# A two-layer AdaLN network on one core: half-chunks at the start of a block, paired products in a correction

## The reference, cut to what matters

```
q = x@Wq + bq;  k = x@Wk + bk;  v = x@Wv + bv
Q = elu(q) + 1; K = elu(k) + 1
KV = sum over tokens of K*v;  Ksum = sum over tokens of K
V = Q * KV / (Q*Ksum + 1e-6)
attn = gelu(V@Wo + bo)
x = layernorm(attn + x) * ln1_s + ln1_b
h = gelu(x@Wf1 + bf1);  ff = gelu(h@Wf2 + bf2)
x = layernorm(ff + x) * ln2_s + ln2_b
```

## Time and profile before

| | us |
|---|---|
| runs | 1975.67, 1970.92, 1968.33 |
| median | 1970.92 |
| profiled execution | 1969.74 |
| its span | 1968.0 |
| TensorE busy | 1720.7 (87%) |
| VectorE busy | 1353.3 (69%) |
| ScalarE busy | 1137.2 (58%) |
| GpSimd busy | 285.7 (15%) |

### The profile page before, as it was taken

How to read it: one execution, slowest core, us unless ns; L and a number is a source line. 1 busy time by engine, 2 the same in 40 slices (tenths; PEclk the granted TensorE clock), 3 DMA queues, 4 the chain that set the end, 5 groups by cost and what they waited for, 6 DMA issues and landing times.

```text
span 1968.0 us, 28168 instructions
## 1 busy us (share of the span) xinstructions
PE 1720.7 (87%) x10420; PEld 770.0 (39%) x10420; DVE 1353.3 (69%) x2656; ACT 1137.2 (58%) x2091; POOL 285.7 (15%) x364
## 2 busy tenths in 40 slices
PE   5898139699999999999979988999989998799999
PEld 4788137122222222222234434444444444444443
DVE  6998876899999999999724356565665656522222
ACT  5465003279989999998863345665566655222222
POOL 4456001400000000000000011111111111111111
PEclk8999658589999999999989989999999999799999
DMA  1000000122100000000012320000000000312441
GB/s 51 1 1 1 0 0 2 39 38 35 17 2 2 2 2 2 2 2 2 18 28 52 91 41 1 17 17 2 15 17 17 17 0 1 43 34 49 48 56 31
DMA packets 72528, 39.12 MB, mean 20 GB/s; under 512 B 22113, under 2 KB 68705, under 8 KB 72401
## 3 DMA queue, kind: packets, MB, share of 16 engines
q1 hardware_dynamic: 71824, 36.65, 10.4%
q10 hardware_dynamic: 576, 0.79, 0.1%
HBM read 34.08 MB, written 3.15 MB: 19 GB/s over the span
## 4 chain that ended last, share of the span: by engine, by line
PE 60%; DVE 28%; ACT 4%; issue 3%; DMA 2%; POOL 1%; SPq 1%; DVEq 0%; ACTq 0%; POOLq 0%
DVE MX L1144 17%; PE PS L1711 6%; PE PS L1226 6%; PE PS L1717 6%; PE PS L2226 4%; PE PS L2227 4%; PE PS L2236 4%; PE PS L1662 4%; PE PS L1252 4%; PE PS L539 3%; PE PS L1681 2%; PE PS L1103 2%; PE PS L1819 2%; DMA SB<-scr_w 2%; DVE MS L643 2%
## 5 line engine op out<-in xcount | busy, mean ns | idle before, releaser
L1285 ACT ACTIVATE tmpb<-PS 128x512 f32<-128x512 f32 x1024 | 554.1, 595 | 76.1 <-PE PS L1252 56.9
L1144 DVE TENSOR_REDUCE MX<-PS 128x2 f32<-128x1024 f32 x512 | 584.5, 1216 | 17.8 <-PE PS L1103 15.9
L1226 PE MATMUL PS<-tmpb,VS 128*32 128x256 f32 x4096 | 327.8, 392 | 1.5 <-ACT tmpb L1285 0.6
L1103 PE MATMUL PS<-KST,QST 56*128 56x512 bf16 x1024 | 205.4, 399 | 18.5 <-DVE MX L1144 16.7
L1252 PE MATMUL PS<-QST,KST 59*128 59x512 bf16 x1024 | 200.6, 388 | 3.8 <-ACT tmpb L1285 1.0
L2261 DVE TENSOR_TENSOR HG<-HG,PS 128x512 f32<-128x512 f32 (+1 forms) x96 | 65.9, 686 | 183.1 <-PE PS L2227 183.1
L2251 ACT ACTIVATE HG<-PS 128x512 f32<-128x512 f32 (+1 forms) x96 | 57.2, 595 | 186.6 <-PE PS L2226 186.6
L1226 PEld LDWEIGHTS PS<-tmpb,VS 128*32 128x32 f32 x4096 | 80.8, 108 | 195.9 <-issue 108.4
L1252 PEld LDWEIGHTS PS<-QST,KST 59*128 59x128 bf16 x1024 | 49.5, 93 | 222.5 <-ACT tmpb L1285 209.0
L1711 PE MATMUL PS<-X,WF 128*128 128x512 f32 x256 | 124.3, 620 | 3.8 <-ACT X L1907 3.7
L1923 ACT ACTIVATE HF<-PS,CL 128x512 f32<-128x512 f32 x128 | 87.9, 687 | 64.6 <-PE PS L1711 64.6
(11 more groups left out here) (335 smaller groups left out, 2528.6 us busy)
## 6 DMA issues: line engine op xcount, KB each, us to landing
SB<-scr_w SPq DMA_DIRECT2D x14, 1024.0 KB, 14.6
WF<-in_L_attn_Wf SPq DMA_DIRECT2D x16, 256.0 KB, 3.1
QST<-NMP SPq DMA_DIRECT2D x192, 1.0 KB
G<-in_L_ffn_w SPq DMA_DIRECT2D x16, 176.0 KB, 2.4
W<-in_L_ffn_w SPq DMA_DIRECT2D x16, 128.0 KB, 2.2
QST<-scr_q SPq DMA_DIRECT2D x14, 128.0 KB
scr_q<-tmpb SPq DMA_DIRECT2D x3, 512.0 KB, 3.6
KST<-scr_k SPq DMA_DIRECT2D x14, 96.0 KB
```

Source lines behind the costliest of these rows:

```text
L1103: pe.matmul(PS[:, b + x, :], QST[r, 2 * g + jj, CH * qc + P * t:CH * qc + P * t + P], KST[r, g, cs(kc)], start=True, stop=True).then_inc(s ...
L1144: r = v.tensor_reduce(MX[:, :, m // (TPC * NC), m // NC % TPC, m % NC], PS[:, b:b + 2, :], AX.X, ALU.max)
L1226: last = pe.matmul(PS[32 * j:32 * j + 32, 3, h], VS[:, kt, u // NC, :], PB[:, kt % 2, j, h], start=(kt == 0 and half == 0), stop=(kt == NT ...
L1285: a.activation(PB[:, kt % 2, j, :], PS[:, at % 3, :], ACT.Exp, scale=HD ** -0.5).then_inc(s_exp, 1)
```

## The change

Two edits in two places.

**Correction.** For every second tile (`paired`) VectorE adds the upper four slices onto the lower four, a sum of 512 elements per row in the same buffer, and TensorE adds up four slices instead of eight.

**Blocks.** Chunk 0 goes from the tanh to the scale and bias in two halves of 256 columns, each with a semaphore step of its own: tanh, projection, gelu, sum, turn (two transposes each), statistics (two of the four), apply and turn back (two each), scale and bias. The halves use two banks: the second half of the projection goes to bank 6, of the turn to bank 0, of the turn back to bank 6. On TensorE the turn of chunk 0 now stands before the projection of chunk 1. The aggregates, the epsilon and the power stay whole. `WARM` is 5. The counts of the semaphores follow: a side-1 counter (`upto1`) has five steps a block instead of four. The second norm is unchanged.

```diff
+        def paired(s):
+            return s % 2 == 1
         def pe_corr(pe, s):
+            n = HD // 2 if paired(s) else HD
...
-            for j in range(HD):
+            for j in range(n):
...
+                m = v.tensor_tensor(CP[s % 3], O[:, s, :, HD:SCOL]...to_broadcast([P, HD, H0, HD]), S0t[:, :, :, :], ALU.mult)
+                if paired(s):
+                    chain.link(m)
+                    h = HD // 2
+                    m = v.tensor_tensor(CP[s % 3][:, 0:h, :, :], CP[s % 3][:, 0:h, :, :], CP[s % 3][:, h:HD, :, :], ALU.add)
+                m.then_inc(s_cp, 1)
...
-        WARM = 6
+        WARM = 5
+        HC, OBANK0B = CH // 2, 6
...
+        def upto1(n):
+            return n + n // NC + 2
...
         def pe_wo(pe, b, c):
+            if c == 0:
+                pe.wait_ge(s_vv, upto1(NC * b) - 1)
+                pe.matmul(PS[:, OBANK[0], 0:HC], WO2[:, :], Q1[:, 0:HC], start=True, stop=True).then_inc(s_wo, 1)
+                pe.wait_ge(s_vv, upto1(NC * b))
+                pe.matmul(PS[:, OBANK0B, 0:HC], WO2[:, :], Q1[:, HC:CH], start=True, stop=True).then_inc(s_wo, 1)
+                return
...
+        def pe_turn_halves(pe, banks, src, ready, count, done):
+            pe.wait_ge(ready, count - 1)
+            for j in range(TPC):
+                if j == TPC // 2:
+                    x.then_inc(done, 1)
+                    pe.wait_ge(ready, count)
+                x = pe.transpose(PS[:, banks[2 * j // TPC], P * j:P * j + P], src[:, P * j:P * j + P], ident[:, :])
+            x.then_inc(done, 1)
...
         def pe_t1(pe, n):
+            if n % NC == 0:
+                pe_turn_halves(pe, (1, 0), Y1, s_y1, upto1(n), s_t1)
+                return
...
         def pe_u1(pe, n):
+            if n % NC == 0:
+                pe_turn_halves(pe, (2, 6), flat(N1), s_n1, upto1(n), s_u1)
+                return
...
             pe_wo(pe, b, 0)
+            pe_t1(pe, n)
             pe_wo(pe, b, 1)
-            pe_t1(pe, n)
...
         def act_v(a, b, c):
+            if c == 0:
+                a.activation(Q1[:, 0:HC], Q1[:, 0:HC], ACT.Tanh, scale=0.5, bias=lnz1[:, 0:1]).then_inc(s_vv, 1)
+                a.activation(Q1[:, HC:CH], Q1[:, HC:CH], ACT.Tanh, scale=0.5, bias=lnz1[:, 0:1]).then_inc(s_vv, 1)
+                return
...
         def act_g1(a, b, c):
+            if c == 0:
+                a.wait_ge(s_wo, upto1(NC * b) - 1)
+                a.wait_ge(s_bo, b + 1)
+                a.activation(ZR[:, 0, 0:HC], PS[:, OBANK[0], 0:HC], ACT.Gelu_apprx_tanh, bias=GB[:, 0:1]).then_inc(s_g1, 1)
+                a.wait_ge(s_wo, upto1(NC * b))
+                a.activation(ZR[:, 0, HC:CH], PS[:, OBANK0B, 0:HC], ACT.Gelu_apprx_tanh, bias=GB[:, 0:1]).then_inc(s_g1, 1)
+                return
...
         def act_x1(a, b, c):
+            if c == 0:
+                if n >= 2:
+                    a.wait_ge(s_y2, upto2(n - 1 - 1))
+                a.wait_ge(s_u1, upto1(NC * b) - 1)
+                a.activation(X1[:, n % 2, 0:HC], PS[:, 2, 0:HC], ACT.Identity, scale=col(b, C1), bias=col(b, B1))
+                a.wait_ge(s_u1, upto1(n))
+                a.activation(X1[:, n % 2, HC:CH], PS[:, 6, HC:CH], ACT.Identity, scale=col(b, C1), bias=col(b, B1)).then_inc(s_bx1, 1)
+                return
...
         def v_y1(v, b, c):
+            if c == 0:
+                v.wait_ge(s_g1, upto1(NC * b) - 1)
+                v.tensor_tensor(Y1[:, 0:HC], ZR[:, 0, 0:HC], HT[:, 0:HC], ALU.add).then_inc(s_y1, 1)
+                v.wait_ge(s_g1, upto1(n))
+                v.tensor_tensor(Y1[:, HC:CH], ZR[:, 0, HC:CH], HT[:, HC:CH], ALU.add).then_inc(s_y1, 1)
+                return
...
+                if halves and j == TPC // 2:
+                    v.wait_ge(turned, counts(side)(n))
+                x = v.bn_stats(BS[:, side, j, :], PS[:, banks[2 * j // TPC], P * j:P * j + P])
...
+                if halves and j == TPC // 2 - 1:
+                    x.then_inc(done, 1)
             x.then_inc(done, 1)
```

More of the change, by code:

```diff
@@ L656, in pe_corr @@
             pe.wait_ge(s_cp, s + 1)
-            for j in range(HD):
-                last = pe.matmul(o, ident[:, :], CP[s % 3][:, j, :, :].rearrange("p h c -> p (h c)"), start=False, stop=j == HD - 1,
+            for j in range(n):
+                last = pe.matmul(o, ident[:, :], CP[s % 3][:, j, :, :].rearrange("p h c -> p (h c)"), start=False, stop=j == n - 1,
                                  skip_group_check=True)
@@ L715, in act_out, with v_corr @@
             act_ht(a, 3)
-        def v_corr(v, c):
+        def v_corr(v, chain, c):
             for s in tiles(c):
@@ L746, in v_out @@
             v.wait_ge(s_ov, NT)
-            v_corr(v, 0)
-            v_corr(v, 1)
+            v_corr(v, chain, 0)
+            v_corr(v, chain, 1)
             v_sums(v, chain, 0)
-            v_corr(v, 2)
+            v_corr(v, chain, 2)
             v_scale(v, chain, 0)
             v_sums(v, chain, 1)
-            v_corr(v, 3)
+            v_corr(v, chain, 3)
             v_scale(v, chain, 1)
@@ L1979, in v_inputs @@
             if b:
-                v_stats(v, chain, 1, 6, s_t2, s_ep2, n - 1)
+                v_stats(v, chain, 1, (6, 6), s_t2, s_ep2, n - 1)
             v_p(v, chain, b, 0)
             if b:
-                v_apply(v, 1, 6, N2, s_r2, s_u2, s_n2, n - 1)
+                v_apply(v, 1, (6, 6), N2, s_r2, s_u2, s_n2, n - 1)
             v_k(v, chain, b, 0)
@@ L2005, in v_y1, with v_stats @@
             n = NC * b + c
-            v.wait_ge(s_g1, n + 1)
+            if c == 0:
+                if n:
+                    v.wait_ge(s_t1, upto1(n - 1))
+                v.wait_ge(s_g1, upto1(NC * b) - 1)
[3 more added lines that the diff above has]
+                return
+            v.wait_ge(s_g1, upto1(n))
             if n:
-                v.wait_ge(s_t1, n)
+                v.wait_ge(s_t1, upto1(n - 1))
             v.tensor_tensor(Y1[:, :], ZR[:, c, :], HT[:, cs(c)], ALU.add).then_inc(s_y1, 1)
-        def v_stats(v, chain, side, bank, turned, done, n):
-            v.wait_ge(turned, n + 1)
+        def v_stats(v, chain, side, banks, turned, done, n, halves=False):
+            v.wait_ge(turned, counts(side)(n) - (1 if halves else 0))
             for j in range(TPC):
-                x = v.bn_stats(BS[:, side, j, :], PS[:, bank, P * j:P * j + P])
+                if halves and j == TPC // 2:
+                    v.wait_ge(turned, counts(side)(n))
+                x = v.bn_stats(BS[:, side, j, :], PS[:, banks[2 * j // TPC], P * j:P * j + P])
             chain.link(x)
@@ L2019, in v_stats, with v_apply @@
             v.tensor_scalar(VE[:, side, :], BA[:, side, :, 1], 1e-6, None, ALU.add).then_inc(done, 1)
-        def v_apply(v, side, bank, N, rstd, used, done, n):
+        def v_apply(v, side, banks, N, rstd, used, done, n, halves=False):
             v.wait_ge(rstd, n + 1)
             if n:
-                v.wait_ge(used, n)
+                v.wait_ge(used, n if side else upto1(n - 1))
             for j in range(TPC):
-                x = v.tensor_scalar(N[:, j, :], PS[:, bank, P * j:P * j + P], BA[:, side, j, 0:1], RR[:, side, j:j + 1],
+                x = v.tensor_scalar(N[:, j, :], PS[:, banks[2 * j // TPC], P * j:P * j + P], BA[:, side, j, 0:1], RR[:, side, j:j + 1],
                                     ALU.subtract, ALU.mult)
+                if halves and j == TPC // 2 - 1:
+                    x.then_inc(done, 1)
             x.then_inc(done, 1)
         def v_first(v, chain, n):
-            v_stats(v, chain, 0, 1, s_t1, s_ep1, n)
+            v_stats(v, chain, 0, (1, 0) if n % NC == 0 else (1, 1), s_t1, s_ep1, n, n % NC == 0)
         def v_body(v, chain, b):
@@ L2042, in v_body @@
                 if m:
-                    v_stats(v, chain, 1, 6, s_t2, s_ep2, n + m - 1)
+                    v_stats(v, chain, 1, (6, 6), s_t2, s_ep2, n + m - 1)
                 if m + 2 < NC:
```

42 lines of the change are left out of this document (23 added, 19 removed).

## The result

| | before | after |
|---|---|---|
| median of the runs, us | 1973.3 (4 runs, 1968.3 to 1976.2) | 1944.62 (4 runs, 1943.6 to 1946.2) |
| ratio, 95% interval | | 0.9861 (0.984 to 0.9881) |
| profiled execution, us | 1969.74 | 1943.64 |
| its span, us | 1968.0 | 1941.8 |

The change is 28.7 us faster by the medians and 26.2 by the two spans. The prediction was 1950, range 1943 to 1960. It was added up from the profiled 1969.74; the median of before had been 1970.92 then and is 1973.3 with a fourth run.

A forecast was written before the change was run, and what follows sets the result against it. TensorE carries 60% of the chain and VectorE 28%; VectorE bounds the softmax stage, TensorE the layer-1 blocks, whose starts are serial. 5.2 + 12.8 + 2.6 = 20.6 us off 1969.74 gives 1949.1, predicted as 1950, range 1943 to 1960.

The forecast's parts named there:

- Correction, 5.2: Layer 0's correction: odd tiles get 5 TensorE products instead of 9, VectorE pays eight sums; 5.2 us less.
- the walk: Step-by-step timing of the correction stage with VectorE as bound, ending at 310.0 instead of 315.17.
- Halves, 12.8: Start of the eight layer-1 bodies: chunk 0 by halves brings the feed-forward 1.6 us earlier each, 12.8 us.
- A cost per instruction speaks against halves: Block start: the skill's objection that small tiles expose a fixed cost; the measured slope's 0.23 us was already counted.
- Warm products, 0: Ahead of each body: five unread products instead of six gain 0, hidden behind VectorE's chain to the weight.
- Clock, 2.6: First feed-forwards of two blocks ran slow at 1.2 GHz; shorter TensorE idle stretches would end this, 2.6 us.
- rival 2: Block starts: the clock's fall moves instead of going; hitting all eight blocks gives 1960 us; chance 0.08.
- Rival 1: Block starts: VectorE and ScalarE queues each 0.4 later, 1956 us; halves as dear as wholes, 1962; chance 0.17 together.
- Rival 3: Block starts: clock falls at the body's start and stays low until the feed-forward's end; 1976 us, chance 0.05.
- Rival 4: Correction gives nothing because VectorE's sum costs as much as it frees; 1954 us, chance 0.06.

The follow-up runs named there:

- filled: Kernel before plus three unread 512-column products on TensorE between projection 3 and the turn back of chunk 0; 1965.94 us, ratio 0.9957.
- blocks_only: Changed kernel with no correction tile paired, so only the blocks changed; 1951.19 us, ratio 0.989 to the kernel before.
- again: The changed kernel itself run once more, in a second set of five runs; 1946.55 us, ratio 0.9878 to the kernel before.
- tanh3_early: Changed kernel with tanh 3 ahead of gelu 1 on ScalarE; 1944.73 us, ratio 0.9863 to the kernel before.
- warm6: Changed kernel with six unread products before the body instead of five; 1948.70 us, ratio 0.9872 to the kernel before.
- corr_only: Kernel before with only the correction paired for odd tiles, blocks as before; 1966.01 us, ratio 0.9967.
- order_only: Kernel before with only chunk 0's turn put ahead of projection 1 on TensorE, no halves; 1971.06 us, ratio 0.9998.
- wo1_first: Changed kernel with TensorE's old order, projection 1 ahead of chunk 0's turn; 1959.76 us, ratio 0.9931 to the kernel before.
- warm0: Changed kernel with no unread products before the body instead of five; 1964.71 us, ratio 0.9948 to the kernel before.
- wo1_filled: Changed kernel with projection 1 ahead of chunk 0's turn and two unread products between projection 3 and the turn back; 1947.88 us, ratio 0.9879.

## Why the prediction was right, step by step

The sign, the places and the range were right. The size was 20.6 us against 28.7 by the medians. The medians can be taken apart in steps: from before to `filled`, which removes the falls only, 7.4 us (8.5 by its own ratio); from `filled` to `blocks_only`, which has the halves, the new order, five unread products ahead instead of six and no fillers, 14.8; from there to the changed kernel, which differs in the pairing alone, 6.6, or 4.6 to `again`. Together 28.7. Since these medians come from different chips, the profiles price the halves and the correction better.

- **Correction, 5.2.** Measured 6.1 on the mean of the stages, 6.7 in the two profiles. The mechanism was right in that fewer products on TensorE are paid for by VectorE until VectorE is the limit. With every tile paired it is (`all_paired`); with every second one the two engines are level, so the walk, which had VectorE as the bound alone, went a little too far. Its prices were a little high. I took 0.74 for a sum and 1.23 for a product; in the row at 302.37 the next product begins 0.60 behind the sum's start, before the sum has ended; the sum itself, which is linked to the product ahead of it, begins only after that product's end (302.33). The walk ended at 31.5 us and the stage at 30.3.
- **Halves, 12.8.** Measured 14.1 (8 × 1.76). The walked lead was 1.6 a block. Half prices were near: gelu 0.45 (0.455), sum 0.42 (0.43), the two scalings together 1.01 (0.92). The error of 0.2 sits in the two queues that the apply waits for. I let the power collide with sum 1 and take 1.25 to 1.4; it took 1.01. And sum 1 ended 5.54 us behind the first tanh instead of the walked 5.73, since its gelu ran 0.2 earlier. In the earlier trace rows sum 1 already runs when the power begins (1389.65 and 1389.82), which I called lying inside it; in the changed kernel it begins 0.33 us after the power has, overlaps it for 0.68 us and lengthens it by nothing. The level queues are there as walked: power and sum 1 end 0.01 us apart. On ScalarE gelu 3 holds the scaling up by 0.2, which `tanh3_early` gives back.
- **A cost per instruction speaks against halves.** The measured halves agree with the slope of the earlier trace rows, 0.455 against 0.45, and not with the lower 0.36, an estimate by the table of the Trainium skill ("VectorE: DVE Perf Modes", the TRN2 errata section). Its advice against small tiles did not decide here: two half gelus took 0.82 us from the start of the first to the end of the second against 0.69 for a whole one, but the first half, for which the sum waits, was done 0.24 earlier than a whole one.
- **Warm products, 0.** `warm6`: 0.09 a block, 0.7 in all.
- **Clock, 2.6.** This is the term that was mis-sized. 2.6 is what the profiled execution of before had lost, and the profiles agree on it (14.9 − 7 × 1.76 = 2.6). The runs lose more, 7 to 9 us by `filled`: about 5 to 6 of the 8.1 us by which the sum fell short. It was read from one execution, and the loss differs between executions: `corr_only` lost 4.8 with the same blocks. The prediction said that the moment decides, in rival 2, and did not conclude that the profile's 2.6 was itself one case of many. It also argued from the length of TensorE's idle stretches, which did shrink to 0.76 us; `order_only` and `wo1_first` show that idle length is not what decides.
- **Rival 1** (level queues, 0.4 each later): did not happen; the queue on VectorE cost nothing and the one on ScalarE 0.2. **Rival 2** (the fall moves): did not happen to this kernel, 0 falls in all 40 bodies of `after`, `again`, `blocks_only`, `all_paired` and `warm6`. It happened to its neighbour `wo1_first`, at 9.7 us, near the 10.4 that rival 2 priced for all eight blocks. **Rival 3** (clock down from the body's start): not with five products; with none, 2.3 a block. **Rival 4**: no.
- **The rest.** 3.2 us of the two profiles' difference lie where nothing was changed (first and third rows of the table of stretches). They are inside the spread of 4.6 us that equal instructions showed, so I take them as luck of this pair of profiles and not as a gain of the change. With `again`, whose profile begins the blocks 1.6 us later, they are 1.7.

One thing stays open: the exact condition under which the clock falls. The column "transposes only" separates the kernels (`warm0`, whose clock fell elsewhere, apart): none of the 72 bodies with 1.6 to 2.4 us fell, and in the four kernels with 2.9 to 4.4 us 17 of 32 did. Within the four it gives no order: 4.4 us went with two and three falls, 3.4 with seven, and these are counts of one profile each. Idle time does not separate them: `order_only` and `wo1_first` idle for 1.5 us at most and fall more often than the kernel before with its 2.75. That fits the Trainium skill ("TensorE: Matmul & The Clock Gate", Part 4: transposes do not count as activity like other products) and its Part 1 (the monitor's window does not start with the kernel), by which equal bodies can differ, as two of eight did in the kernel before. No run here replaced the transposes themselves, so it was not shown that they are the cause; that products in the stretch end the falls was shown, by `filled` and `wo1_filled`.

## What to carry to other kernels

Where one chain crosses several engines and all of them idle, price the halves by the slope between two sizes of the same operation in the trace, and then walk each engine's queue: the lead is what the later of two queues leaves. When TensorE has idle stretches, read what it does in them and where its real products stand, not only how long it idles; an order that looks 0.2 us worse or better can cost or save 10 us by the clock. A loss by the clock read in one profile is one case of many, so count it as a range, and look at the spread of the runs of before.

## What the runs showed of the hardware that I had not expected

- Whether projection 3 ends 4.9 us behind the bias product (`wo1_first`) or 6.3 (the changed kernel) went with seven falls or none: 9.7 us. In `tanh3_early` it ends at 5.5, and none fell.
- In `wo1_first` the falls followed one another: the first feed-forwards went from 4.79 to 5.38 us, the spacing settled at 61.4, and every body behind the first one that fell did too. That a fall brings on the next was not tested.
- Kernels with equal instructions ahead of the blocks reach them at 1187.75 to 1192.3 us. In the two profiles at the ends, the changed kernel and `wo1_first`, the correction's first product was already 1.5 us apart (277.4 and 278.9); from 190.8 to 194.2 the granted clock was 1.00 in the first and 0.50 in the second.
- GpSimd's power of four columns takes 1.01 us where VectorE is at rest when it begins (176 of 176 such powers in the fourteen profiles). Where VectorE's sum of two SBUF operands is already running, the power ends 0.86 to 0.87 us behind the end of that sum (272 of 272), so it takes 1.39 when it begins 0.17 us into the sum and 1.54 when it begins 0.02 us in. A sum that begins 0.33 us after the power, as in the changed kernel, lengthens neither: 1.01 and 0.69, with 0.68 us of overlap. What counts is which of the two begins first.
